# Involution phase: the last image's partial sums added by VectorE and GpSimd, and the first image's taps 2 and 3 placed ahead of the next image's kernel products

## The reference

```python
def _L1_conv_ref(x, w_v, w1, gn_gamma, gn_beta, w2, b2):     # x is layer-normalised over channels
    t = relu(group_norm(d4_1x1(x, w1), gn_gamma, gn_beta, cmid))
    wgt = einsum('oi,bighw->boghw', w2, t...) + b2           # 9 weights for each pixel and each of 8 channels of a group
    ...
    xv = d4_1x1(x, w_v)                                      # the values
    pats = unfold_patches(xv, 3)                             # 3 x 3 neighbourhoods, zero at the border
    return (wv * pats).sum(axis=4)                           # sum over the 9 taps
...
x = x + _L1_conv_ref(_ln_c(x), ...)
```

## Time and profile before

| what | us |
| --- | --- |
| median of 3 runs | 1245.9 |
| lowest, highest run | 1243.61, 1249.0 |
| the profiled execution, its own time | 1249.48 |
| its span, first to last instruction | 1247.6 |
| mean granted TensorE clock in it | 0.933 of full speed |

### The profile page before, as it was taken

One profiled execution on the slowest core, in us unless ns is written; L12 is line 12 of the kernel. 1 busy time (PEld: TensorE's weight loads), 2 busy tenths in 40 slices (PEclk: granted clock), 3 DMA queues, 4 the chain that ended last, 5 costly groups with the idle time before them and its releaser, 6 DMA issues. The chain is left out here.

```text
span 1247.6 us, 34991 instructions
## 1 busy us (share of the span) xinstructions
PE 1079.2 (86%) x9969; PEld 732.6 (59%) x9970; DVE 892.2 (72%) x2124; ACT 797.0 (64%) x2043; POOL 541.8 (43%) x422
## 2 busy tenths in 40 slices
PE   6869979888689999999999999379999999845698
PEld 2324435444379999999999999234444444312464
DVE  3672338877767777777877777239999999953587
ACT  5865559997657777777777777256666566502375
POOL 0000005757736533333333333428988898970000
PEclk9989989999789999999999999689999999965599
DMA  6200004321213211111111111212455545343000
GB/s 209 71 1 0 0 3 139 101 86 51 67 53 102 78 45 49 45 47 43 43 40 41 41 45 39 76 31 68 87 120 130 128 112 114 85 101 103 0 1 35
DMA packets 65357, 82.04 MB, mean 66 GB/s; under 512 B 10537, under 2 KB 51133, under 8 KB 65136
## 3 DMA queue, kind: packets, MB, share of 16 engines
q1 hardware_dynamic: 51696, 46.96, 12.7%
q0 software_dynamic: 13568, 33.78, 10.9%
HBM read 36.60 MB, written 28.88 MB: 52 GB/s over the span
## 5 line engine op out<-in xcount | busy, mean ns | idle before, releaser
L558 ACT ACTIVATE Y<-ps 128x256 f16<-128x256 f32 x584 | 224.3, 384 | 127.2 <-PE ps L512 93.6
L604 DVE SCALAR_TENSOR_TENSOR Y<-ps,Y 128x256 f16<-128x256 f32 x584 | 241.8, 422 | 45.5 <-ACT Y L558 38.0
L455 POOL DMA_INDIRECT expert_out<-Y x152 | 149.5, 984 | 273.3 <-DVE Y L624 242.8
L492 PE MATMUL ps<-Y,weights 128*128 128x128 f16 x1168 | 213.0, 220 | 6.7 <-DVE Y L604 5.5
L493 PE MATMUL ps<-Y,weights 128*128 128x128 f16 x1168 | 212.8, 220 | 0.0
L496 PE MATMUL ps<-Y,weights 128*128 128x128 f16 x1168 | 212.8, 220 | 0.0
L510 PE MATMUL ps<-weights,Y 128*128 128x128 f16 x1160 | 210.0, 219 | 0.0
L511 PE MATMUL ps<-weights,Y 128*128 128x128 f16 x1160 | 210.0, 219 | 0.0
L512 PE MATMUL ps<-weights,Y 128*128 128x128 f16 x1160 | 209.9, 219 | 0.0
L1111 POOL DMA_INDIRECT dispatched<-d_rows,slot x128 | 128.5, 1004 | 160.8 <-ACT t_sq L858 110.6
L1241 POOL TENSOR_TENSOR iv_pool_sum<-iv_pool_sum,iv_pool_part 128x1024 f32<-128x1024 f32 x80 | 193.2, 2415 | 9.8 <-DVE iv_pool_part L1459 3.3
(11 more groups left out here) (324 smaller groups left out, 2226.5 us busy)
## 6 DMA issues: line engine op xcount, KB each, us to landing
Y<-dispatched SPq DMA_DIRECT2D x152, 65.5 KB
X<-x SPq DMA_DIRECT2D x16, 512.0 KB, 4.3
iv_got<-expert_out SPq DMA_DIRECT2D x16, 512.0 KB, 4.1
X<-iv_pool_sum POOLq DMA_DIRECT2D x16, 512.0 KB, 4.5
X<-iv_own_sum POOLq DMA_DIRECT2D x16, 512.0 KB, 4.5
out<-X SPq DMA_DIRECT2D x16, 512.0 KB, 3.0
Y<-w_moe SPq DMA_DIRECT2D x8, 512.0 KB
expert_out<-Y POOLq DMA_INDIRECT x152, 2.3
```

The costliest lines, as they stand in the source:

```text
L455: pool.indirect_dma_start(env.yt, bass.IndirectOffsetOnAxis(ap=token[:, k:k + 1], axis=0), result[:, k, :], None, bounds_check=TOKENS - 1, ...
L492: pe.matmul(out, high, xh, start=True, stop=False)
L558: act.activation(hh[e][:, part_cols[h]], hidden[e][h], ACT.Relu).then_inc(hi_ready[e], 1)
L604: dve.scalar_tensor_tensor(hl[e][:, cols], hidden[e][h], 0.0, hh[e][:, cols], ALU.max, ALU.subtract).then_inc(h_split[e], 1)
```

## The change

Three edits, all in `phase_involution`:

1. The last image is not joined by DMA. VectorE, behind its loop, waits for its own pair sum and adds own_sum to X for image 15. GpSimd, behind its loop, waits for that and for its own last sum, and adds pool_sum to X. The two joins of image 15 fall away.
2. SyncE's last send waits for GpSimd's add (`pool_summed` at 16 x 6 + 1) instead of `own_joined`.
3. In image 0, TensorE issues taps 2 and 3 directly behind tap 1, ahead of `kernels(1)` and `values(1, 0)`. `values(1, 1)` and `group(1)` then follow directly, ahead of tap 4. The other images keep their order.

```diff
             def send(n):
-                sp.wait_ge(S["own_joined"], n * 16 + 16)
+                if isinstance(n, int) and n == IMAGES - 1:
+                    sp.wait_ge(S["pool_summed"], IMAGES * POOL_ADDS + 1)
+                else:
+                    sp.wait_ge(S["own_joined"], n * 16 + 16)
                 sp.dma_start(out[:, bass.ds(n * PIX, PIX)], image(X, n)).then_inc(S["sent"], 16)
...
-                join_pool(n, q)
+                if not isinstance(n, int) or n < IMAGES - 1:
+                    join_pool(n, q)
 
             images(pool, body)
-            join_own(IMAGES - 1, (IMAGES - 1) % 2)
+            last = IMAGES - 1
+            pool.wait_ge(S["summed"], IMAGES * OWN_ADDS + 1)
+            pool.wait_ge(S["pool_summed"], IMAGES * POOL_ADDS)
+            pool.tensor_tensor(grid(image(X, last)), grid(image(X, last)), pool_sum[last % 2][:, :, :], ALU.add).then_inc(S["pool_summed"], 1)
...
                     tap(n, q, 1)
+                    tap(n, q, 2)
+                    tap(n, q, 3)
                 if ahead >= 1:
                     kernels(n + 1)
                     values(n + 1, 0)
                 if not first:
                     tap(n, q, 1)
-                tap(n, q, 2)
+                    tap(n, q, 2)
                 if ahead >= 1:
                     values(n + 1, 1)
-                tap(n, q, 3)
+                if not first:
+                    tap(n, q, 3)
                 if ahead >= 1:
                     group(n + 1)
                 tap(n, q, 4)
...
             images(dve, body)
+            last = IMAGES - 1
+            dve.wait_ge(S["summed"], IMAGES * OWN_ADDS)
+            dve.tensor_tensor(grid(image(X, last)), grid(image(X, last)), own_sum[last % 2][:, :, :], ALU.add).then_inc(S["summed"], 1)
```

## The result

| | kernel before | changed kernel |
| --- | --- | --- |
| median, us (runs) | 1245.57 (6) | 1235.12 (6) |
| lowest, highest | 1243.61, 1249.0 | 1234.37, 1237.77 |
| profiled execution, its span | 1249.48, 1247.6 | 1234.37, 1232.5 |
| mean granted clock in it | 0.933 | 0.944 |

The ratio is 0.9917 [0.9902, 0.9931]: faster by 10.4 us, with the interval 8.6 to 12.2. The forecast of 1239.0 was 3.9 us too high, inside its range. The rest of this document is about those 3.9 us, and about which steps of the sum were right.

The account below looks back on a forecast made before the run. The TensorE, VectorE, ScalarE chain sets the loop's pace, and 13.3 us lie bare at the involution's end. End 7.6 - 1.2 = 6.4, plus first image 0.5, is 6.9 us off the median 1245.9: 1239.0 us, range 1234.0 to 1243.0.

Parts of the forecast that it names:

- The end without a collision: End of the involution: two DMA joins and their waits replaced by adds, 10.25 - 2.48 - 0.15 = 7.6 us gained.
- Rival (d): End of the involution: the next phase doesn't wait for it, only 0.5 us remains, 1245.4 us; chance 0.04.
- The first image: Image 0: taps 2 and 3 earlier move VectorE's idle from product 2 to product 4, 0.5 us gained.
- (b): Image 0: ScalarE's chain holds the split, so nothing gained or 0.27 us lost, 1239.5 to 1239.8 us; chance 0.14.
- (c): Image 0: shorter wait before tap 4 gives much more, up to 7.6 + 4.2 = 11.8 us, 1234.1 us; chance 0.06.
- The collision: End of the involution: VectorE's new add with two SBUF operands and a GpSimd sum exclude each other, costing 1.2 us.
- Rival (a): End of the involution: no exclusion between the two adds, 7.6 + 0.5 = 8.1 us gained, 1237.8 us; chance 0.23.
- Slower (e): Images 1 and 2: a TensorE pause in image 0 lowers its clock, losing 17 us, 1256.5 us; chance 0.03.

Follow-up runs that it names:

- e2: Kernel before with only the new order in image 0, the last image still joined by DMA: 1244.13 us (12 runs), ratio 1.0.
- e7: Changed kernel with image 0's tap 4 also put ahead of the group matmul: 1236.98 us in one execution.
- e4: Kernel before, unaltered, profiled and timed a second time: 1245.28 us (12 runs), ratio 0.9999.
- e3: Changed kernel with VectorE's add to X held until GpSimd's fourth sum is done, a half-size add in front: 1237.0 us (8 runs), ratio 0.9929.
- e5: Changed kernel, VectorE's add held until GpSimd's fourth sum, own sum made in PSUM so each add has one SBUF operand: 1237.19 us, one execution.
- e8: Changed kernel; for the last image GpSimd sums products 0 to 3, VectorE gathers its part and products 4 to 6 in PSUM: 1232.18 us, ratio 0.9908.
- e9: e8 with image 0's tap 4 also ahead of the group matmul: 1231.5 us (5 runs), ratio 0.9901.
- e6: Changed kernel; for the last image GpSimd sums products 0 to 3, VectorE adds products 4 to 6 to its own sum: 1233.54 us, ratio 0.9905.

## Why the prediction was right and wrong

**The end without a collision: right.** 7.6 was forecast, 7.74 measured. GpSimd's add with the gap in front took 1112.45 - 1109.97 = 2.48, the forecast to the digit; only the hand-over to SyncE was smaller, 0.02 instead of 0.15. Rival (d) is out: the gate phase followed the send by the same 3 us.

**The first image: right, with its mechanism.** Moved to the time of before (plus 6.03), the group matmul runs at 840.49 (forecast 840.5), product 4 begins at 841.77 (841.7), the split at 845.47 (845.4); 0.44 arrive instead of 0.5. The same 0.4 came with e2 alone. Rivals (b) and (c) are out; e7 shows that ScalarE's chain stops (c).

**The collision: this step failed.** It was to cost 1.2 us and cost 0.10. Two things were wrong in it. The first is the place. The prediction's "it is released at 1109.5, in the middle of a GpSimd sum" was read from the earlier trace rows, and those carry the clock of that one execution: it had fallen to 0.50 at 1095 to 1100, and VectorE's pair sum ended 0.74 us behind the start of GpSimd's fourth sum. The same kernel's second profile, e4, has a clock of 1.00 at 1085 to 1100, and there the pair sum ends 0.91 us ahead of the fourth sum:

```profile
1103.40 1.22 DVE L1467 TENSOR_TENSOR iv_own_sum<-ps,iv_own_part 128x1024 f32<-128x1024 f32 x1
1105.53 7.60 POOL L1241 TENSOR_TENSOR iv_pool_sum<-iv_pool_sum,iv_pool_part 128x1024 f32<-128x1024 f32 x3
```

So the place was that of one execution with a low clock; e7, the one other profile with a low clock there, has it late too, by 0.9 us. In the changed kernel the clock stays up:

```profile
1090.00:1095.00 5.00, 4.32 (x18) 1.24 (x16) 5.00 (x5) 0.00 (x0) 4.25 (x4) 1.00 0.30 113
1095.00:1100.00 5.00, 3.26 (x13) 0.93 (x12) 5.00 (x5) 0.00 (x0) 4.71 (x3) 1.00 0.51 97
```

The pair sum ended at 1101.34, 0.93 us ahead of the fourth sum, and the add (1101.38 to 1102.81) met the end of the third sum at 1101.73. It waited for it, and ended 1.08 us behind it, just as in e3. But here this cost GpSimd almost nothing, since it issues a DMA from 1101.67 on and begins its fourth sum only at 1102.27: 7.70 for the three sums instead of 7.60. The second is the size: where the add begins well inside a sum and another sum follows at once (e3, e7), the collision costs 0.8. By the Trainium skill, SBUF — State Buffer, "Who interferes with whom", the one that comes later is blocked for the whole of the other, and a VectorE instruction with at most one SBUF input isn't; e3 agrees with the first for VectorE (it ends 1.08 us behind the sum that it met), e5 with the second (1.22 us beside a sum).

Rival (a), 8.1 us with no exclusion, comes out right in size, but its reason was wrong: the exclusion exists, and the add was held by it; it only fell where GpSimd had a DMA to issue. So its size is right by luck.

**What the sum lacked.** With 0.10 for 1.2 the sum is 8.0, and the four stretches show 8.1. So of the 3.9 us by which the forecast was too high, 1.2 are the sum's, 0.3 come from the kernel before (1245.57 on six runs, 1245.9 on three), and 2.3 aren't in the involution; against the pooled 9.1 that last part is 1 us. Some is in the last phase: 117.0 us in the changed kernel against 117.6 and 118.0. Stretches of it in the changed kernel, then in e4_before_again:

```profile
1160.00:1168.00 8.00, 4.22 (x17) 3.39 (x17) 2.76 (x17) 3.30 (x7) 0.00 (x0) 0.50 0.00 0
1168.00:1171.00 3.00, 1.82 (x5) 0.85 (x4) 0.24 (x1) 1.57 (x4) 0.00 (x0) 0.68 0.00 0
1171.00:1180.00 9.00, 8.53 (x37) 5.66 (x37) 7.97 (x21) 6.35 (x15) 0.00 (x0) 1.00 0.01 3
```

```profile
1179.00:1182.00 3.00, 1.12 (x5) 0.62 (x3) 0.36 (x1) 1.46 (x4) 0.00 (x0) 0.94 0.00 0
1183.00:1186.00 3.00, 3.00 (x9) 2.21 (x8) 2.12 (x6) 1.59 (x4) 0.00 (x0) 0.50 0.01 3
1187.00:1190.00 3.00, 3.00 (x15) 2.27 (x14) 2.66 (x7) 2.44 (x6) 0.00 (x0) 1.00 0.03 5
```

In the change the granted clock rises some 54 us behind the phase's start and stays at 2.4 GHz until 3 us before the end; in e4_before_again it rises at 53, falls at 56 to the 1.2 GHz level and rises again at 60. Of the nine profiles with a new end, six have the first course and 116.9 to 117.1 us; e3 has the second and 117.76, as have e4 and e2 (117.6 and 117.7), which have the old end; e8 and e9 rise only at 59.4 and take 118.2, much like the first profile of the kernel before (59.7, 117.98). So no part of the change sets it alone. Five of the six profiles with the change's hand-over have the first course, and none of the three with the old one, so the change may favour it; what decides it stays open, and no run was made for it. In e8 and e9 it goes the other way and hides 1.2 us of their gain. The rest of the difference lies in earlier stages, which differ as much between profiles of one kernel, such as the preparation, 29.03 us in the first profile and 25.7 in the next of the kernel before.

**Slower (e)** didn't come: the clock in image 0 stays up, and the loop takes 243.6 us in all profiles.

## What to carry to other kernels

Where a phase ends in a string in which only one thing runs, the string can be priced from its own rows; here two accumulating DMAs in a row were worth 7.7 us, and 7.6 was forecast. A collision between two engines is a matter of places that shift with the clock, here by up to 1.7 us, so price it as a chance and not as a term, or take it out by giving the VectorE instruction an operand in PSUM. A pause that is taken away from one product stands before the next one unless what that waits for moves too: follow it until a wait for another engine ends it.

## What the hardware showed that I had not expected

VectorE's fp32 add of 128x1024 with both operands in SBUF takes 1.23 us alone (e6) and 2.85 to 3.75 when it begins inside a GpSimd add or just before it (e3, e6, e7). Wherever it begins, it ends 1.08 to 1.09 us behind the instruction that it met, in the changed kernel as well, and a GpSimd sum that follows at once pays 0.8 only. An accumulating DMA of 512 KB within SBUF takes 4.5 us from issue to landing, and the plain store behind it, of as much, 2.6. And the granted clock has courses of its own: the same kernel's preparation took 29.03 and 25.71 us in two profiles, and in the changed kernel it took 25.99.
